# Attention with a mixture of experts on one Trainium2 core: row sums of squares moved from ScalarE's accumulator to two halvings on GpSimd and a reduction on VectorE

## The chip, the core and the metric

The kernel runs on one core of one Trainium2 chip. The metric is the device time of one execution in microseconds; a lower one is better. The kernel before took 217.38 us (median of 3 runs, 215.89 to 218.58).

The core's engines run side by side, each through its own list of instructions in the order in which the program wrote it. TensorE (PE in the profile) multiplies matrices into the banks of PSUM. ScalarE (ACT) and VectorE (DVE) read PSUM and SBUF. GpSimd (POOL) works on SBUF alone and issues the indirect DMAs. SyncE (SP) issues the other DMAs. Engines wait for one another by semaphores; an engine that waits holds up all that stands behind the waiting instruction in its list.

## The reference

```python
x = L0_attn_x                                        # (8, 512, 128), f32
mod = (_silu(L0_c) @ L0_wmod).reshape(8, 6, 1, -1)   # sa, ca, ga, sb, cb, gb
h = _layernorm(x) * (1 + ca) + sa
x = x + ga * attn(h)
h = _layernorm(x) * (1 + cb) + sb
x = x + gb * ffn(h)                                  # top-1 routing to 16 experts, 128 -> 512 -> 128

# attn(x), with rms_norm(x) = x * rsqrt(mean(x * x, axis=-1) + eps)
qkv = einsum('btd,ed->bte', rms_norm(x), w_qkv)
q, k, v = split(qkv, 3, axis=-1)
q, k = rms_norm(q), rms_norm(k)
w = exp(k); kv = w * v
y = sigmoid(q) * cumsum(kv, axis=1) / (cumsum(w, axis=1) + 1e-06)
u, g = split(einsum('bte,fe->btf', y, w_swiglu), 2, axis=-1)
return x + einsum('btd,ed->bte', u * silu(g), w_out)
```

The change touches one thing in it: the sums of squares of q and of k over their 128 channels, which the rms_norm of q and k needs.

## The kernel before

The work is 8 batches of 512 tokens; a batch is four tiles (`NJ` = 4) of 128 tokens. The attention and the routing of all batches come first and end with the scatter of the routed rows to DRAM (`scatter`, L495, 32 indirect DMAs on GpSimd). Eight pairs of experts follow, which this change doesn't touch; they start when all rows are scattered.

In the attention part each engine has a list of calls `name(b)` written out by hand, b being the batch (GpSimd L510 to L517, ScalarE L652 to L673, VectorE L926 to L951, TensorE L1193 to L1215). Batches overlap in these lists. The chain of one batch is:

1. `normalize1(b)` (GpSimd or VectorE) gives the normed rows, `transpose1(b)` (TensorE) transposes them to bank 2, and `modulate1(b)` (ScalarE or VectorE, L301) scales and shifts them into `hT`, 128 channels by 512 tokens.
2. `squares(b)` (GpSimd, L482) squares `hT`, and `h_square_sums(b)` (TensorE, L1025) sums the squares; `h_means(b)` (VectorE, L742) reads them.
3. `project_qk(b)` (TensorE, L1033) fills banks 0 and 1 with q and k: for each tile j 128 columns of q and 128 of k, so a bank holds two tiles. There is one such pair of banks, and `project_qk(b+1)` waits until `exp_q(b)` has read it.
4. `square_sums(b)` (ScalarE, L554) makes `ssq`, the eight sums of squares of every row, and `qk_means(b)` (VectorE, L751) makes `nrm` of them (one instruction, L754).
5. `rms_scales(b)` (ScalarE, L564) takes `nrm` through Ln and Exp; `exp_k(b)` and `exp_q(b)` (ScalarE, L571, L580) read q and k from PSUM with these scales.
6. `transpose_k`, `transpose_q`, `weigh_v`, `transpose_kv`, the cumulative sums `scan_w` and `scan_kv` (VectorE), `denominator`, `log_denominator`, `reciprocal` and `weigh_sums` (GpSimd or VectorE, L271) give y.
7. `project_g`, `project_u`, `clamp_g`, `exp_g`, `log_g`, `sigmoid_g`, `silu`, `gate_u`, `project_out` and `residual` end the attention; the second layer norm, the logits, `count_seen` and `slots` lead to `scatter(b)`.

`square_sums(b)` before is eight pairs, one for each half tile:

```python
last = act.activation(junk[:, 2 * j + m, :], ps_qk[:, j, m * D:(m + 1) * D],
                      ACT.Square, accum_out=ssq[:, j, m:m + 1])
```

Each pair is an ACTIVATE of 128x128 and an ACTIVATION_READ_ACCUMULATOR of 128x1. TensorE's list has a few multiplications without use (`run_early`, `run_late`) that fill gaps. The order on GpSimd around the change is `squares(0); normalize1(1); squares(1); weigh_sums(0); squares(2); silu(0); squares(3); normalize1(4); squares(4); normalize1(5); squares(5); weigh_sums(3); silu(2); count_seen(0); normalize1(6); scatter(0); squares(6); normalize1(7)` and so on.

Of the kernel before, what the change touches and what calls it, by code (L numbers as in the profile page):

```python
# [5 lines left out]
def adaln_attention_moe(  # L6
# [30 lines left out]
    ALU = mybir.AluOpType  # L37
    ACT = mybir.ActivationFunctionType
    X = mybir.AxisListType.X
# [23 lines left out]
    with ctx:  # L63
# [3 lines left out]
        def sem(name):  # L67
            return ctx.enter_context(nc.semaphore(name))
# [129 lines left out]
        yw = junk[:, 0:NS, :]  # L198
        x_tiles = x_all[:, :, :, :].rearrange("p b j d -> p (b j) d")
# [35 lines left out]
        pool_past = sem("pool_past")  # L235
        last_sent = sem("last_sent")
# [222 lines left out]
        def _(pool):  # L459
# [22 lines left out]
            def squares(b):  # L482
                after(pool, hT_done, b)
                after(pool, mh_ps, b, 1)
                pool.tensor_tensor(hsq[:, :], hT[b % NHT][:, :], hT[b % NHT][:, :], ALU.mult  # L485
                                   ).then_inc(hsq_done, 1)

            def count_seen(b):

                after(pool, oh_done, b)  # L490
                after(pool, rank_ps, b)
                pool.tensor_tensor(seen[:, :, :], seen[:, :, :], oh[b % 2][:, :, :], ALU.add
                                   ).then_inc(seen_done, 1)
# [16 lines left out]
            squares(0); normalize1(pool, 1); squares(1); weigh_sums(pool, 0)  # L510
            squares(2); silu(pool, 0); squares(3); normalize1(pool, 4); squares(4)
            normalize1(pool, 5); squares(5); weigh_sums(pool, 3); silu(pool, 2); count_seen(0)
            normalize1(pool, 6); scatter(0); squares(6); normalize1(pool, 7); silu(pool, 3)
            weigh_sums(pool, 4); squares(7); count_seen(1); scatter(1); weigh_sums(pool, 5)
# [29 lines left out]
        def _(act):  # L544
# [9 lines left out]
            def square_sums(b):  # L554
                after(act, nrm_b, b, 1)
                for j in range(NJ):
                    if j % 2 == 0:
                        after(act, qk_ps, 2 * b + j // 2)
                    for m in range(2):
                        last = act.activation(junk[:, 2 * j + m, :], ps_qk[:, j, m * D:(m + 1) * D],  # L560
                                              ACT.Square, accum_out=ssq[:, j, m:m + 1])
                last.then_inc(ssq_done, 1)
# [91 lines left out]
            reciprocal(0); rms_scales(1); exp_k(1); exp_q(1); keep_row(0); ln1_scale(3); exp_g(0)  # L654
            log_g(0); sigmoid_g(0); keep_row(1); modulate1(act, 3); log_denominator(1); square_sums(2)
            ln1_scale(4); reciprocal(1); rms_scales(2); exp_k(2); exp_q(2); exp_g(1); ln2_scale(0)
            keep_row(2); log_g(1); sigmoid_g(1); square_sums(3); ln1_scale(5); rms_scales(3); exp_k(3)
            exp_q(3); keep_row(3); log_denominator(2); reciprocal(2); square_sums(4)
            log_denominator(3); modulate2(act, 0); rms_scales(4); exp_k(4); exp_g(2); exp_q(4)
# [59 lines left out]
        def _(dve):  # L719
# [31 lines left out]
            def qk_means(b):  # L751
                after(dve, ssq_done, b)
                dve.wait_ge(nrm_a, b + 1)
                dve.scalar_tensor_tensor(nrm[:, 0:2 * NJ].rearrange("p (j m) -> p j m", m=2), ssq[:, :, :],  # L754
                                         1.0 / D, mh[:, :].unsqueeze(2).to_broadcast([P, NJ, 2]),
                                         ALU.mult, ALU.add).then_inc(nrm_b, 1)
# [171 lines left out]
            normalize1(dve, 2); scan_kv(0); h_means(1); qk_means(1); modulate1(dve, 2); diagonal(0); aggregate1(3)  # L928
# [3 lines left out]
            clamp_g(1); scan_w(2); modulate1(dve, 4); weigh_v(2); aggregate1(5); shift2(0); stats1(6)  # L932
            silu(dve, 1); gate_u(1); qk_means(3); denominator(2); h_means(4); shift1(5)
            normalize2(dve, 0); scan_kv(2); residual(1); scan_w(3); weigh_sums(dve, 2)
            modulate1(dve, 5); denominator(3); weigh_v(3); qk_means(4); clamp_g(2); stats2(1)
# [432 lines left out]
```

## Time and profile before

| what | us |
|---|---|
| median of 3 runs | 217.38 |
| lowest and highest | 215.89, 218.58 |
| span of the profiled execution | 217.0 |
| attention and routing, up to the last scatter's issue | 0 to 129.4 |
| experts | some 130 to 217 |

The profile is one execution. Its span runs from the first to the last instruction and lies 0.4 us under the median of the runs. PE is TensorE's matrix multiplications (their ends are modelled, so a busy PE isn't PE at its peak), PEld its loads of weights. A row of the timeline has the start in us, the duration in us, the engine, the line, the operation, output and input, the count, and in brackets the idle time of the engine before it with what ended that. Consecutive instructions of an engine can overlap at their ends, so the distance of two starts is the price in a list, and is a little less than the duration.

### The profile page before, as it was taken

Reading aid. Unit: us, or ns where it says so; the run is one execution under the profiler, and the core shown is the slowest. Engines: PE = TensorE matmul, PEld = TensorE weight load, DVE = VectorE, ACT = ScalarE, POOL = GpSimd, SP = SyncE. Lnnn points to the kernel's source line nnn. Section 1 sums busy time; section 2 is a strip of 40 time slices with the busy share of each in tenths; the row PEclk is TensorE's granted clock in tenths of the full one; section 3 lists DMA queues with packets and bytes.
Section 4 is the critical chain, followed back from the end, with each engine's and each line's share of the span. In section 5 each row is a group of like instructions: output and inputs, shape, how many; then the busy total and the mean of one; then the engine's idle time right before and its main releaser. Section 6 shows DMA issues by size and latency. Waiting matters only on the chain.

```text
span 217.0 us, 4034 instructions
## 1 busy us (share of the span) xinstructions
PE 192.2 (89%) x1177; PEld 155.3 (72%) x1177; DVE 153.2 (71%) x476; ACT 145.0 (67%) x425; POOL 113.8 (52%) x139
## 2 busy tenths in 40 slices
PE   6999599999999979999988749999999999999930
PEld 4789377788879759775665414888878889788830
DVE  3657999999999999999996407156847668485430
ACT  4494868999999979987756641574855848555300
POOL 6311504431387828577767760002754378487774
PEclk9788999999999999999999996999999999999996
DMA  5999999507905013114453216999879585321000
GB/s 149 285 343 360 355 360 309 222 5 215 270 21 177 0 53 147 48 73 138 161 186 119 99 65 159 362 358 357 277 254 283 168 268 157 85 100 46 31 30 20
DMA packets 37284, 38.60 MB, mean 178 GB/s; under 512 B 2591, under 2 KB 31334, under 8 KB 37264
## 3 DMA queue, kind: packets, MB, share of 16 engines
q1 hardware_dynamic: 33936, 31.29, 46.1%
q0 software_dynamic: 3328, 7.07, 9.1%
q8 instruction: 9, 0.15, 0.3%
q14 instruction: 11, 0.09, 0.1%
HBM read 19.19 MB, written 18.95 MB: 176 GB/s over the span
## 4 chain that ended last, share of the span: by engine, by line
PE 59%; DVE 17%; issue 8%; POOL 7%; ACT 4%; DMA 2%; POOLq 1%; SPq 0%; DVEq 0%
PE bank L1280 14%; PE bank L1266 11%; PE bank L1039 5%; POOL out_dram L529 4%; PE bank L1083 3%; PE bank L1109 3%; PE bank L1057 3%; PE bank L1092 2%; PE bank L1078 2%; PE bank L1094 2%; PE bank L1050 2%; DVE kvsum L780 2%; PE bank L1327 2%; PE bank L1237 2%; DVE rows L804 2%
## 5 line engine op out<-in xcount | busy, mean ns | idle before, releaser
L529 POOL DMA_INDIRECT out_dram<-x_all,rest x40 | 43.2, 1080 | 42.2 <-DVE x_all L985 23.8
L503 POOL DMA_INDIRECT dispatched_rows<-rows,slot x32 | 32.2, 1006 | 16.0 <-issue 9.0
L709 ACT ACTIVATE HT<-bank 128x320 f32<-128x320 f32 x64 | 28.0, 438 | 10.2 <-PE bank L1266 9.8
L1280 PE MATMUL bank<-HT,w 128*128 128x320 f32 x112 | 32.4, 432 | 0.0
L1280 PEld LDWEIGHTS bank<-HT,w 128*128 128x128 f32 x112 | 20.6, 189 | 6.7
L1266 PE MATMUL bank<-xth,w1h 128*128 128x320 f32 x64 | 22.6, 353 | 0.2 <-DVE xtl L961 0.2
L955 DVE TENSOR_TENSOR w1l<-w,w1h 128x1024 fp32r<-128x1024 f32 x8 | 16.1, 2022 | 7.4 <-DMA dispatched_rows<-rows,slot 7.4
L1004 DVE COPY OT<-bank 128x320 f32<-128x320 f32 x14 | 6.9, 492 | 18.5 <-PE bank L1280 18.5
L1266 PE MATMUL bank<-xth,w1l 128*128 128x320 f32 x64 | 19.8, 309 | 0.0
L1266 PE MATMUL bank<-xtl,w1h 128*128 128x320 f32 x64 | 19.8, 309 | 0.0
L560 ACT ACTIVATE junk<-bank 128x128 f32<-128x128 f32 x64 | 16.5, 288 | 1.5 <-PE bank L1039 1.3
L485 POOL TENSOR_TENSOR hsq<-hT 128x512 f32<-128x512 f32 x8 | 9.3, 1164 | 15.2 <-ACT hT L308 9.6
L1039 PE MATMUL bank<-wqkvT,hT 128*128 128x256 f32 x64 | 16.5, 405 | 0.0
L681 ACT CAST w1h<-w 128x1024 fp32r<-128x1024 f32 x8 | 16.3, 2044 | 0.0
L694 ACT CAST xth<-bank 128x640 fp32r<-128x640 f32 x7 | 4.8, 692 | 15.8 <-PE bank L1237 15.8
L977 DVE SCALAR_TENSOR_TENSOR junk<-bank,rest 128x128 f32<-128x128 f32 x40 | 11.5, 345 | 5.4 <-PE bank L1299 3.6
L1057 PE MATMUL bank<-ident,ewkv 128*128 128x128 f32 x96 | 14.7, 280 | 0.0
L1057 PEld LDWEIGHTS bank<-ident,ewkv 128*128 128x128 f32 x96 | 11.9, 148 | 3.8 <-issue 2.2
L277 POOL TENSOR_TENSOR yT<-kvsum,rden 128x512 f32<-128x512 f32 x6 | 7.6, 1273 | 13.0 <-ACT rden L596 12.5
L1039 PEld LDWEIGHTS bank<-wqkvT,hT 128*128 128x128 f32 x64 | 12.7, 206 | 2.4 <-issue 0.5
L560 ACT ACTIVATION_READ_ACCUMULATOR junk<-bank 128x1 f32 x64 | 14.2, 222 | 0.0
L1092 PE MATMUL bank<-diag_ga,hT 128*128 128x128 f32 x64 | 12.8, 282 | 0.6 <-DVE GT L800 0.6
(172 smaller groups left out, 494.1 us busy)
## 6 DMA issues: line engine op xcount, KB each, us to landing
w<-in_L_ffn_w_dram SPq DMA_DIRECT2D x16, 512.0 KB, 7.6
dispatched_rows<-blank SPq DMA_DIRECT2D x8, 965.0 KB, 13.2
rest<-dispatched_rows SPq DMA_DIRECT2D x8, 645.0 KB, 6.4
hin<-dispatched_rows SPq DMA_DIRECT2D x7, 320.0 KB, 7.5
x_all<-in_L_attn_x_dram SPq DMA_DIRECT2D x8, 256.0 KB, 5.2
rows<-gb_row SPq DMA_DIRECT2D x8, 256.0 KB, 3.8
out_dram<-rows SPq DMA_DIRECT2D x8, 256.0 KB, 3.2
out_dram<-x_all,rest POOLq DMA_INDIRECT x40, 2.3
```

Source lines behind the costliest of these rows:

```text
L503: pool.indirect_dma_start(out=disp_d, out_offset=bass.IndirectOffsetOnAxis(ap=slot[:, b, j:j + 1], axis=0), in_=rows[:, b, j, :], in_offse ...
L529: pool.indirect_dma_start(out=out_d.rearrange("b t d -> (b t) d"), out_offset=bass.IndirectOffsetOnAxis(ap=rest[i % RING][:, n, C_TOK - D: ...
L560: last = act.activation(junk[:, 2 * j + m, :], ps_qk[:, j, m * D:(m + 1) * D], ACT.Square, accum_out=ssq[:, j, m:m + 1])
L681: act.copy(w1h[i % 2][:, :, :, :], w1[i % RING][:, :, :].rearrange("p e (m f) -> p e f m", f=NF)).then_inc(w1h_done, 1)
L709: act.activation(HT[e][:, f, :], ps_h[c % HB][:, 0:CAP], ACT.Gelu_apprx_tanh).then_inc(h_done, 1)
L955: dve.tensor_tensor(w1l[i % 2][:, :, :, :], w1[i % RING][:, :, :].rearrange("p e (m f) -> p e f m", f=NF), w1h[i % 2][:, :, :, :].bitcast( ...
L977: last = dve.scalar_tensor_tensor(yw[:, n, :], ROWS[n] if i == LAST else ps_y[:, n * D:(n + 1) * D], rest[i % RING][:, n, C_PROB - D:C_PRO ...
L1039: last = pe.matmul(ps_qk[:, j, :], hT[b % NHT][:, j * P:(j + 1) * P], wqkvT[:, 0:2 * D], start=True, stop=True)
L1057: last = pe.transpose(ps[:, j * P:(j + 1) * P], t[:, j, m, :], ident[:, :])
L1092: pe.matmul(ps_u[:, j * P:(j + 1) * P], hT[b % NHT][:, j * P:(j + 1) * P], diag_ga[:, b, :], start=True, stop=False)
L1266: last = pe.matmul(ps_h[c % HB][:, 0:CAP], w[i % 2][:, e, f, :], x[i % 2][:, e * CAP:(e + 1) * CAP], start=(n == 0), stop=(n == 2))
L1280: last = pe.matmul(ps_o[e], w2[i % RING][:, e, f, :], HT[e][:, f, :], start=(f == 0), stop=(f == NF - 1))
```

## The change

It does two things.

`square_sums(b)` no longer uses the accumulator. ScalarE squares a whole bank at a time (two ACTIVATEs of 128x512 instead of eight pairs) into `junk`, which then holds 8 rows of 128 squares in each partition. GpSimd's new `fold_squares(b)` adds the upper 64 of each row to the lower 64, waits for that, and adds the upper 32 to the lower 32. `qk_means(b)` on VectorE first reduces 8 rows of 32 to `ssq` (a new TENSOR_REDUCE), waits for it, and then goes on as before. `fold_squares(b)` has its place written out in GpSimd's list.

`modulate1(b)` for b = 2, 4 and 5 moves from VectorE's list to ScalarE's: for 2 it stands between `reciprocal(0)` and `rms_scales(1)`, for 4 between `ln2_scale(0)` and `keep_row(2)`, for 5 between `square_sums(4)` and `log_denominator(3)`. TensorE's list and SyncE's are the same.

```diff
+        squared = junk[:, :, :].rearrange("p (h n) d -> p h (n d)", h=2)
...
+        sqr_done = sem("sqr_done")
+        fold_a, fold_b = sem("fold_a"), sem("fold_b")
...
+            def fold_squares(b):
+
+                after(pool, sqr_done, b)
+                pool.tensor_tensor(junk[:, :, 0:64], junk[:, :, 0:64], junk[:, :, 64:128], ALU.add
+                                   ).then_inc(fold_a, 1)
+                pool.wait_ge(fold_a, b + 1)
+                pool.tensor_tensor(junk[:, :, 0:32], junk[:, :, 0:32], junk[:, :, 32:64], ALU.add
+                                   ).then_inc(fold_b, 1)
...
-            squares(0); normalize1(pool, 1); squares(1); weigh_sums(pool, 0)
-            squares(2); silu(pool, 0); squares(3); normalize1(pool, 4); squares(4)
-            normalize1(pool, 5); squares(5); weigh_sums(pool, 3); silu(pool, 2); count_seen(0)
-            normalize1(pool, 6); scatter(0); squares(6); normalize1(pool, 7); silu(pool, 3)
-            weigh_sums(pool, 4); squares(7); count_seen(1); scatter(1); weigh_sums(pool, 5)
+            squares(0); normalize1(pool, 1); fold_squares(0); squares(1); fold_squares(1); weigh_sums(pool, 0)
+            squares(2); silu(pool, 0); fold_squares(2); squares(3); normalize1(pool, 4); squares(4)
+            fold_squares(3); normalize1(pool, 5); fold_squares(4); squares(5); weigh_sums(pool, 3)
+            silu(pool, 2); fold_squares(5); count_seen(0); normalize1(pool, 6); scatter(0); squares(6)
+            normalize1(pool, 7); fold_squares(6); silu(pool, 3); weigh_sums(pool, 4); squares(7)
+            count_seen(1); scatter(1); fold_squares(7); weigh_sums(pool, 5)
...
             def square_sums(b):
-                after(act, nrm_b, b, 1)
-                for j in range(NJ):
-                    if j % 2 == 0:
-                        after(act, qk_ps, 2 * b + j // 2)
-                    for m in range(2):
-                        last = act.activation(junk[:, 2 * j + m, :], ps_qk[:, j, m * D:(m + 1) * D],
-                                              ACT.Square, accum_out=ssq[:, j, m:m + 1])
-                last.then_inc(ssq_done, 1)
+                after(act, ssq_done, b, 1)
+                for half in range(2):
+                    after(act, qk_ps, 2 * b + half)
+                    last = act.activation(squared[:, half, :], bank01[:, half * 512:(half + 1) * 512], ACT.Square)
+                last.then_inc(sqr_done, 1)
...
-            reciprocal(0); rms_scales(1); exp_k(1); exp_q(1); keep_row(0); ln1_scale(3); exp_g(0)
+            reciprocal(0); modulate1(act, 2); rms_scales(1); exp_k(1); exp_q(1); keep_row(0); ln1_scale(3); exp_g(0)
...
-            keep_row(2); log_g(1); sigmoid_g(1); square_sums(3); ln1_scale(5); rms_scales(3); exp_k(3)
+            modulate1(act, 4); keep_row(2); log_g(1); sigmoid_g(1); square_sums(3); ln1_scale(5); rms_scales(3); exp_k(3)
...
-            log_denominator(3); modulate2(act, 0); rms_scales(4); exp_k(4); exp_g(2); exp_q(4)
+            modulate1(act, 5); log_denominator(3); modulate2(act, 0); rms_scales(4); exp_k(4); exp_g(2); exp_q(4)
...
             def qk_means(b):
-                after(dve, ssq_done, b)
+                after(dve, fold_b, b)
+                dve.tensor_reduce(ssq[:, :, :].rearrange("p j m -> p (j m)"), junk[:, :, 0:32], X, ALU.add
+                                  ).then_inc(ssq_done, 1)
+                dve.wait_ge(ssq_done, b + 1)
                 dve.wait_ge(nrm_a, b + 1)
...
-            normalize1(dve, 2); scan_kv(0); h_means(1); qk_means(1); modulate1(dve, 2); diagonal(0); aggregate1(3)
+            normalize1(dve, 2); scan_kv(0); h_means(1); qk_means(1); diagonal(0); aggregate1(3)
...
-            clamp_g(1); scan_w(2); modulate1(dve, 4); weigh_v(2); aggregate1(5); shift2(0); stats1(6)
+            clamp_g(1); scan_w(2); weigh_v(2); aggregate1(5); shift2(0); stats1(6)
...
-            modulate1(dve, 5); denominator(3); weigh_v(3); qk_means(4); clamp_g(2); stats2(1)
+            denominator(3); weigh_v(3); qk_means(4); clamp_g(2); stats2(1)
```

## Rows read from the trace of the kernel before

**Rows 1.** Windows: stretch, length, busy us of PE, PEld, DVE, ACT, POOL, granted clock, DMA.
```profile
16.00:18.00 2.00, 2.00 (x11) 2.00 (x10) 0.89 (x1) 1.22 (x4) 1.04 (x1) 0.50 1.06 362
...
41.00:49.00 8.00, 8.00 (x53) 6.69 (x52) 7.91 (x28) 7.65 (x34) 2.93 (x5) 1.00 0.06 20
...
60.00:70.00 10.00, 9.99 (x73) 8.56 (x71) 9.65 (x37) 9.90 (x39) 8.01 (x12) 1.00 0.31 108
...
14.00:98.00 84.00, 78.52 (x535) 64.83 (x534) 78.95 (x262) 72.85 (x276) 40.82 (x51) 0.98 0.55 179
```
**Rows 2.** Waits, 10 to 140 us: us in total, times, longest.
```profile
PE bank L1190 <- DVE diag_ga L920: 2.1, 1, 2.1
PE bank L1083 <- DVE rows L804: 2.0, 3, 1.5
...
ACT nrl L566 <- DVE nrm L754: 1.0, 3, 0.5
```
**Rows 3.** Timeline of ScalarE, batches 1, 3 to 5.
```profile
20.92 0.26 ACT L560 ACTIVATE junk<-bank 128x128 f32<-128x128 f32 x1
...
22.91 0.68 ACT L596 ACTIVATE rden<-lden 128x512 f32<-128x512 f32 x1
...
47.11 1.16 ACT L584 ACTIVATE ewkv<-bank,nrr 128x128 f32<-128x128 f32 x4
...
49.30 0.63 ACT L596 ACTIVATE rden<-lden 128x512 f32<-128x512 f32 x1
49.84 0.26 ACT L560 ACTIVATE junk<-bank 128x128 f32<-128x128 f32 x1
...
63.37 0.24 ACT L566 ACTIVATE nrl<-nrm 128x12 f32<-128x12 f32 x1
...
63.84 0.78 ACT L308 ACTIVATE hT<-bank,mod 128x512 f32<-128x512 f32 x1
64.52 1.13 ACT L576 ACTIVATE ewkv<-bank,nrr 128x128 f32<-128x128 f32 x4
```
**Rows 4.** Groups by line in 0 to 140 us: busy us, mean ns of one.
```profile
L284 POOL TENSOR_TENSOR gs<-gc,sg 128x512 f32<-128x512 f32 x4 | 5.1, 1272 | 5.4 <-ACT sg L612 5.3
...
L794 DVE TENSOR_SCALAR gc<-bank 128x512 f32<-128x512 f32 x8 | 5.5, 685 | 0.6 <-issue 0.3 <-PE bank L1078 0.2
...
L831 DVE TENSOR_REDUCE mx<-bank 128x4 f32<-128x64 f32 x8 | 1.7, 219 | 1.9 <-PE bank L1109 1.8
...
L649 ACT COPY gb_row<-bank 128x512 f32<-128x512 f32 x2 | 1.2, 600 | 0.0
```
**Rows 5.** Timeline of GpSimd, four places, and the last scatter.
```profile
33.50 1.04 POOL L485 TENSOR_TENSOR hsq<-hT 128x512 f32<-128x512 f32 x1
...
60.77 1.76 POOL L294 TENSOR_SCALAR xh<-x_all,rs,nm 128x128 f32<-128x128 f32 x4
...
68.12 1.05 POOL L485 TENSOR_TENSOR hsq<-hT 128x512 f32<-128x512 f32 x1
...
73.80 1.04 POOL L485 TENSOR_TENSOR hsq<-hT 128x512 f32<-128x512 f32 x1
...
128.45 0.97 POOL L503 DMA_INDIRECT dispatched_rows<-rows,slot  x1 [0.30 <-issue]
```
**Rows 6.** Timeline of VectorE: the sums' consumer in batches 1 and 6, and a diagonal.
```profile
23.11 0.17 DVE L754 SCALAR_TENSOR_TENSOR nrm<-ssq,mh 128x8 f32<-128x8 f32 x1 [0.41 <-ACT junk L560]
...
23.91 2.11 DVE L920 TENSOR_TENSOR diag_ga<-ident,mod 128x1024 f32<-128x1024 f32 x1
...
73.86 1.02 DVE L754 SCALAR_TENSOR_TENSOR nrm<-ssq,mh 128x8 f32<-128x8 f32 x1
```
**Rows 7.** Timeline of TensorE: two sums of squares of h, and the projection of batch 4.
```profile
36.27 0.95 PE L1029 MATMUL bank<-tri,hsq 128*128 128x1 f32 x8
...
48.41 1.96 PE L1039 MATMUL bank<-wqkvT,hT 128*128 128x256 f32 x8
...
69.59 0.95 PE L1029 MATMUL bank<-tri,hsq 128*128 128x1 f32 x8
```

## Prediction

> **What bounds the kernel now.** I read the windows by stage first. In 14 to 98 us, where the change lies, TensorE is busy 78.5 of 84 us, VectorE 79.0, ScalarE 72.9 and GpSimd only 40.8 [rows 1]. That invites moving work to GpSimd. The single stages say more: in 41 to 49 us TensorE has 8.00 of 8, VectorE 7.91 and ScalarE 7.65, in 60 to 70 us 9.99, 9.65 and 9.90 of 10 [rows 1]. Three engines are full at once, each through a list in fixed order. Such a kernel is bound by the chain that passes from list to list, and an engine's total is not its limit. The waits say the same: few are long, and ScalarE waits for VectorE's `nrm` for 1.0 us in all [rows 2]. So the sums of squares are now made just in time for what needs them. Nor is GpSimd free everywhere: in 60 to 70 us it is busy 8.01 of 10 us [rows 1], as the first scatter lies there. After the attention the experts wait for the last scatter, issued at 128.45 us [rows 5]. They take the rest of the span whatever came before, so a delay of the attention is a delay of the kernel.
>
> **Prices, one batch.** On ScalarE the eight pairs last from 20.92 to 22.91 us, 1.99 us [rows 3]. A 128x512 read of a bank has a mean of 0.60 us there, and successive starts of that size lie 0.54 us apart (49.30 to 49.84) [rows 3, 4]. Two Squares then cost 1.04 to 1.2; I take 1.04, so ScalarE's list gets 0.95 us shorter, 7.6 us over eight batches. Three modulations come onto it at 0.68 us each (63.84 to 64.52) [rows 3]: +2.0. VectorE gives about as much for those three and takes on eight reductions.
>
> The path is another matter. Before, from the first square to the start of `nrm` it was 23.11 - 20.92 = 2.19 us [rows 3, 6]. Now come the Squares (1.1 to the end of the second), two folds and a reduction, with a semaphore between each.
> - First fold, 512 outputs from two inputs: GpSimd's nearest row has 1.27 [rows 4]; with both inputs the same tile it has 1.04 [rows 5]. I take 1.27, since the two halves are different data, and 1.04 as the lower bound.
> - Second fold, 256 outputs: not in the trace. Below it lies a 128x128 instruction at 1.76 / 4 = 0.44 [rows 5], above it 1.27. I take 0.7, nearer the lower end, since it has half the elements.
> - Reduction of 256 to 8: below 0.22 (64 elements), above 0.69 (512) [rows 4]; on the line between them 0.42.
> - Four hand-overs between engines or behind a semaphore at some 0.07 each, worked out from 63.37 + 0.24 to 63.84 and the like: 0.25.
>
> The sum is 1.1 + 1.27 + 0.7 + 0.42 + 0.25 = 3.75, 1.55 longer than before. The bounds give 3.1 (0.9 longer) and 4.6 (2.4 longer). Seen from ScalarE, `rms_scales(b)` can start 2.85 us after its last Square (with 0.2 for `nrm`), less what its list has in between. The Trainium skill (GPSIMD Engine Reference, section 3.1) gives a two-input elementwise instruction about 2.6 cycles for each element on GpSimd; taking 256 elements off the 1.27 by that rule, an estimate of mine for the second fold is 0.72, and the sum would be the same.
>
> **One more price: the port.** `nrm` reads two SBUF tiles and has 0.17 us in batch 1 but 1.02 in batch 6, started at 73.86, just behind GpSimd's squares at 73.80 and ended with them [rows 5, 6]. So it stands still while GpSimd reads. After the change the instruction in front of which GpSimd finished its fold is exactly what sets `nrm` free, and GpSimd goes on at once with `weigh_sums`, `squares` or `silu` (1.04 to 1.27); the reduction hides 0.45 of that, so `nrm` is 0.6 to 0.8 later wherever GpSimd has such work ready: batches 1, 2, 4, 6, 7. The Trainium skill (SBUF — State Buffer, section "Who interferes with whom") states it as a rule: a VectorE instruction with two SBUF inputs blocks against a GpSimd instruction that reads SBUF for the whole of it, and a reduction doesn't. The trace agrees for `nrm`; no row here has a reduction against GpSimd.
>
> **The walk.** I followed the lists by hand, with each instruction behind the last of its waits and the trace's durations kept. Delays against before:
> - Batch 0 has nothing between `square_sums` and `rms_scales`. VectorE stands until the folds are done; +1.0 at 20 us, as part of it ran in ScalarE's idle time.
> - Batch 1: the modulation and `reciprocal(0)` cover 1.2 of 2.85. VectorE's `diagonal(0)`, which ended at 26.0 [rows 6] and for which TensorE stood 2.1 us [rows 2], waits for `nrm`, and `weigh_sums(0)` behind the fold blocks it further: +0.6, together 1.6.
> - Batch 2: `squares(3)` ran at 33.50 on GpSimd and TensorE took it at 36.27, so it had 1.7 us to spare [rows 5, 7]. Now it stands behind `fold_squares(2)`, which waits for Squares that end at about 36.3. Folds to 38.3, squares to 39.4, TensorE stands until then: 36.27 becomes 39.5. +1.6, together 3.2. All queued behind on TensorE (project_g(1), project_qk(3)) goes with it.
> - Batch 3: only `ln1_scale` (0.47, like the pair 63.37 to 63.84) [rows 3] lies between: 2.85 - 0.47 - 0.2 of old wait - 0.95 saved = +1.2, together 4.4. The exp_q that starts at 47.11 ends at 48.27, and TensorE's project_qk(4) starts at 48.41 [rows 3, 7]. There is no slack in that loop: 48.4 becomes 52.8.
> - Batch 4: modulate1(5), a logarithm and a modulate2 cover 1.9; with the port and the moved instruction +0.7, together 5.1.
> - Batch 5: `normalize1(6)` ran at 60.77, beside the squares [rows 5]. Now it is behind `fold_squares(5)` and `count_seen(0)`, and starts at about 68.4: +7.7. After it stand scatter(0) with its four DMAs and squares(6), which goes from 68.12 to some 75.7; TensorE's 69.59 becomes 76.8 [rows 5, 7]. modulate1(6) (63.84) [rows 3] waits for the transpose of normalize1(6), so ScalarE is held up too. +2.0, together 7.1.
> - Batch 6: ScalarE has over 3 us of other work in between. The fold lies in front of `silu(3)` and `weigh_sums(4)`, whose delay TensorE's old wait for `residual` (1.5) [rows 2] takes up. +0.
> - Batch 7: `log_denominator` alone (0.54) is cover: +1.3, with `weigh_sums(5)` on the port +0.7; together 9.1.
> - The tail has small waits of several engines (of the 2.0 of TensorE for `residual`, 0.5 is left) [rows 2]: I give back 1.1.
>
> Sum: +8.0. The profiled span is 217.0, so 225.0; the median is 0.4 above the span: 225.4. SyncE's transfers are issued as before; the first experts' weights are in long before. Where I cost the reductions on VectorE at nothing beyond the path, it is because VectorE is waiting for the folds at that point; otherwise eight of them less three modulations cost 8 x 0.45 - 3 x 0.72 = 1.4 us.
>
> **Rivals.**
> 1. ScalarE is the bound and the folds are covered. For it: ScalarE has 9.90 of 10 us in 60 to 70 us [rows 1], and all of its squares there follow the instruction before without a gap. Then 7.6 - 2.0 = 5.6 us come off: 211.8. It decides if `rms_scales(b)` finds `nrm` ready, that is if 2.85 us of other work stands before it in the list; that holds in one batch of eight. Chance 0.10.
> 2. Gains and waits cancel: the folds at their lower bounds (path +0.9), and GpSimd's order costs nothing since VectorE or ScalarE is later there anyway. ScalarE's 2.85 becomes 2.2 and batch 3's +1.2 becomes +0.6; four such batches (0, 1, 3, 7) give 2.4: 219.8. Chance 0.08.
> 3. Only the list of ScalarE counts, not that of GpSimd: the batch 2 and 5 terms (3.6) drop out: 221.8. Against it: squares(3)'s margin of 1.7. Chance 0.12.
> 4. More than forecast: TensorE's clock. After its early waits it was granted 0.50 in 16 to 18 us, the level of 1.2 GHz, though the 2.1 us for which TensorE waited for the diagonal [rows 2] left the mean of 14 to 98 us at 0.98 [rows 1]. New waits of 1 to 2 us could bring two such stretches, each costing about 2: 229.5. The upper bounds of the folds (0.85 more in five batches) give the same. Chance 0.10.
> 5. The forecast, 221.8 to 229: chance 0.60.
>
> **How the numbers follow.** 2% is 4.3 us, so slower begins at 221.7, which is also about what a measurement of this kernel can tell. Slower: 0.60 + 0.10 + half of rival 3 = 0.76. Within 2%: 0.08 + 0.06 = 0.14. Faster: 0.10. The range reaches from 220, which leaves out rivals 1 and 2, to 231 (the upper bounds and a little clock).
>
> **What would show it.** ScalarE's idle time in front of L566's counterpart should be some 10 us in all, released by VectorE's `nrm`; VectorE's in front of the reduction some 8, released by the second fold; TensorE's sum of squares of batch 3 should stand at about 39.5 and wait for GpSimd; project_qk(4) at about 52.8; the last scatter at about 136.5. Squares under 1.2 us a batch and folds of 1.27 and 0.7 show the prices. I am wrong if those waits are there but the last scatter is not later (then the chain was elsewhere), or if the folds take under 1.5 us together.

## The result, and the profile after

The changed kernel took 234.44 us (median of 4 runs, 231.73 to 235.33), the kernel before 217.98 beside it (4 runs, 215.89 to 219.60). The ratio is 1.073, with an interval of 1.0665 to 1.0795: slower by 16.5 us at the medians, 15.9 by the ratio, where +8.0 was forecast. Ratios leave disturbed runs out (of the kernel after, the profiled one of 235.33 us), so what one kernel costs over another is taken from ratios below, at 218 us for 1.00, and can differ by an us or two from the medians shown. The profiled execution has a span of 233.2 us, 16.2 over the 217.0 of before.

The groups by line in 0 to 146 us (busy us, mean ns of one, then idle time before them and its releaser) stand against [rows 3, 4, 6]:

```profile
L494 POOL TENSOR_TENSOR junk<-junk 128x512 f32<-128x512 f32 x8 | 10.1, 1267 | 14.5 <-ACT junk L571 14.5
...
L571 ACT ACTIVATE junk<-bank 128x512 f32<-128x512 f32 x16 | 8.8, 586 | 3.1 <-PE bank L1052 3.1
...
L497 POOL TENSOR_TENSOR junk<-junk 128x256 f32<-128x256 f32 x8 | 5.8, 723 | 0.6
...
L767 DVE SCALAR_TENSOR_TENSOR nrm<-ssq,mh 128x8 f32<-128x8 f32 x8 | 3.9, 484 | 0.3
...
L763 DVE TENSOR_REDUCE ssq<-junk 128x8 f32<-128x256 f32 x8 | 3.3, 418 | 5.5 <-POOL junk L497 5.3
...
L576 ACT ACTIVATE nrl<-nrm 128x12 f32<-128x12 f32 x8 | 1.7, 210 | 14.8 <-DVE nrm L767 14.8
```

The prices are those of the forecast: 1.27, 0.72 and 0.42 us, and two Squares within 1.06. The last row is where the chain shows: ScalarE stands 14.8 us for `nrm`, against 1.0 before [rows 2]. GpSimd stands as long, 14.5 us, for the Squares, and all that is queued behind the first fold stands with it. The waits in 10 to 146 us (total, times, longest) tell who pays for that on TensorE, against [rows 2]:

```profile
PE bank L1091 <- POOL yT L280: 3.2, 2, 2.0
...
PE bank L1042 <- POOL hsq L488: 2.7, 2, 1.9
PE bank L1203 <- DVE diag_ga L933: 2.6, 1, 2.6
...
ACT rden L606 <- POOL yT L280: 2.2, 1, 2.2
```

GpSimd's timeline and TensorE's show one of these places, the sum of squares of batch 3, as [rows 5, 7] do for before:

```profile
39.81 1.27 POOL L494 TENSOR_TENSOR junk<-junk 128x512 f32<-128x512 f32 x1 [3.49 <-ACT junk L571]
41.16 0.72 POOL L497 TENSOR_TENSOR junk<-junk 128x256 f32<-128x256 f32 x1
41.84 1.04 POOL L488 TENSOR_TENSOR hsq<-hT 128x512 f32<-128x512 f32 x1
```
```profile
28.32 2.08 PE L1203 MATMUL bank<-diag_ga,wout 128*128 128x512 f32 x2 [2.59 <-DVE diag_ga L933]
30.18 1.91 PE L1091 MATMUL bank<-yT,wswT 128*128 128x512 f32 x2
31.89 1.91 PE L1096 MATMUL bank<-yT,wswT 128*128 128x512 f32 x2
...
42.93 1.05 PE L1042 MATMUL bank<-tri,hsq 128*128 128x1 f32 x8 [1.94 <-POOL hsq L488]
...
88.44 2.05 PE L1091 MATMUL bank<-yT,wswT 128*128 128x512 f32 x2 [1.97 <-POOL yT L280]
```

`squares(3)` needs nothing of the folds, yet it stands behind two of them and behind the 3.5 us for which the first waits. TensorE stands 1.94 us for it. Behind each of the three waits something further happens, which the windows show (columns as in [rows 1]; the granted clock is the figure after POOL's):

```profile
24.00:28.00 4.00, 1.13 (x8) 0.97 (x8) 2.50 (x6) 1.70 (x6) 3.92 (x4) 0.88 1.06 361
28.00:32.00 4.00, 3.68 (x5) 1.62 (x6) 3.58 (x14) 2.81 (x11) 1.16 (x1) 0.50 1.06 358
...
44.00:48.00 4.00, 4.00 (x11) 1.89 (x12) 2.00 (x12) 1.60 (x7) 1.19 (x3) 0.57 0.00 0
...
88.00:92.00 4.00, 3.56 (x11) 2.53 (x12) 2.85 (x10) 2.98 (x10) 1.64 (x3) 0.57 0.00 2
...
132.00:136.00 4.00, 3.96 (x21) 2.45 (x21) 2.84 (x12) 2.27 (x6) 2.83 (x4) 0.61 0.41 148
```

In 28 to 32 us TensorE is busy 3.68 of 4 us but does 5 multiplications: its granted clock is 0.50, the level of 1.2 GHz. In the timeline above, two pairs of 128x512 start 1.71 us apart (30.18, 31.89). At full clock they start 0.86 apart (23.82 and 24.68, in e2's timeline below). So these three waits cost themselves, and then about as much again in slow multiplications. A fourth slow stretch, at 132 us, stands behind a wait of 1.39 us. Not every such wait has one behind it: before's of 2.1 us for the diagonal [rows 2] ended at 26.07, and its windows of 24 to 28 and 28 to 32 us both have 1.00.

How the delay grew, against the forecast and against a version with the clock kept (run e3, below), in us:

| mark | before | forecast | after | e3 |
|---|---|---|---|---|
| sum of squares of batch 3 starts | 36.27 | 39.5 | 42.93 | 38.23 |
| project_qk(4) starts | 48.41 | 52.8 | 58.19 | 51.95 |
| normalize1(6) on GpSimd starts | 60.77 | 68.4 | 73.80 | 67.62 |
| sum of squares of batch 6 starts | 69.59 | 76.8 | 82.02 | 75.84 |
| last scatter is issued | 128.45 | 136.5 | 145.63 | 137.74 |

From that issue to the end of the span it is 88.6 us before, 87.6 after and 88.2 in e3, so the delay is made in the attention. (The 129.4 of the table of stages is where that last instruction ends.)

### The profile page after: what moved, and what is told of

Same layout as the page of the kernel before. It is cut to its first block, busy times and chain, and to the rows that moved or that the text cites. A ratio compares the mean times of both kernels' runs of the same rounds, so it can differ in the third digit from the quotient of the medians.

```text
span 233.2 us, 3946 instructions
## 1 busy us (share of the span) xinstructions
PE 199.6 (86%) x1177; PEld 158.7 (68%) x1177; DVE 158.0 (68%) x481; ACT 139.2 (60%) x316; POOL 129.5 (56%) x155
## 4 chain that ended last, share of the span: by engine, by line
PE 48%; DVE 14%; POOL 14%; issue 11%; ACT 8%; DMA 2%; POOLq 1%; DVEq 0%; ACTq 0%
PE bank L1293 13%; PE bank L1279 11%; POOL out_dram L542 4%; POOL junk L494 4%; PE bank L1052 4%; PE bank L1091 3%; PE bank L1096 3%; ACT junk L571 2%; PE bank L1203 2%; POOL dispatched_rows L515 2%; DVE w1l L968 2%; POOL junk L497 2%; PE bank L1250 2%; DVE ewkv L776 2%; DVE rows L817 1%
## 5 line engine op out<-in xcount | busy, mean ns | idle before, releaser
L494 POOL TENSOR_TENSOR junk<-junk 128x512 f32<-128x512 f32 x8 | 10.1, 1267 | 14.5 <-ACT junk L571 14.5
L1052 PE MATMUL bank<-wqkvT,hT 128*128 128x256 f32 x64 | 17.0, 413 | 0.5 <-ACT ewkv L594 0.5
L1070 PE MATMUL bank<-ident,ewkv 128*128 128x128 f32 x96 | 14.5, 278 | 2.4 <-ACT ewkv L586 2.4
L1091 PE MATMUL bank<-yT,wswT 128*128 128x512 f32 x16 | 11.3, 798 | 3.5 <-POOL yT L280 3.2
L1105 PE MATMUL bank<-diag_ga,hT 128*128 128x128 f32 x64 | 13.3, 290 | 0.0
L1279 PEld LDWEIGHTS bank<-xth,w1h 128*128 128x128 f32 x64 | 12.1, 188 | 1.3 <-DVE xtl L974 0.6
```

The costliest lines, as they stand in the source:

```text
L494: pool.tensor_tensor(junk[:, :, 0:64], junk[:, :, 0:64], junk[:, :, 64:128], ALU.add).then_inc(fold_a, 1)
L1052: last = pe.matmul(ps_qk[:, j, :], hT[b % NHT][:, j * P:(j + 1) * P], wqkvT[:, 0:2 * D], start=True, stop=True)
L1070: last = pe.transpose(ps[:, j * P:(j + 1) * P], t[:, j, m, :], ident[:, :])
L1091: pe.matmul(ps_g, wswT[:, D:2 * D], yT[:, :], start=True, stop=True).then_inc(g_ps, 1)
L1105: pe.matmul(ps_u[:, j * P:(j + 1) * P], hT[b % NHT][:, j * P:(j + 1) * P], diag_ga[:, b, :], start=True, stop=False)
L1279: last = pe.matmul(ps_h[c % HB][:, 0:CAP], w[i % 2][:, e, f, :], x[i % 2][:, e * CAP:(e + 1) * CAP], start=(n == 0), stop=(n == 2))
```

## The experiments

Theories: *path*, the chain from the Squares through the folds to `nrm` is longer and ScalarE waits for it; *list*, what counts is the useful work on GpSimd behind a fold that waits; *clock*, the new waits lower TensorE's clock; *port*, GpSimd's reads of SBUF hold VectorE up. A diff against the kernel before is marked so; the others are against the kernel after. "Before" is the median of its runs beside each experiment.

### The three modulations

**e1**: they go back to VectorE.

```diff
-            reciprocal(0); modulate1(act, 2); rms_scales(1); exp_k(1); ...
+            reciprocal(0); rms_scales(1); exp_k(1); ...
...
-            normalize1(dve, 2); scan_kv(0); h_means(1); qk_means(1); diagonal(0); aggregate1(3)
+            normalize1(dve, 2); scan_kv(0); h_means(1); qk_means(1); modulate1(dve, 2); diagonal(0); aggregate1(3)
```
(batches 4 and 5 alike)

> The changed kernel with the three modulations back in VectorE's list; squares, folds and reduction stay. Path theory (the 3.75 us from the first square to nrm makes the delay, wherever the modulations are): ScalarE gets 2.0 us shorter, VectorE 2.1 us longer while it mostly waits for folds; the time stays within 1.5 us of the changed kernel's 234. Rival (the modulations overload ScalarE in batches 4 and 5): 3 us or more come off, 231 or less. Clock theory: TensorE's long waits are for the diagonal, for squares(3) and for weigh_sums(4), none of which this takes away, so the three stretches at half clock stay.

Measured 233.29 us (233.06 to 236.24), ratio 1.0774 [1.0658, 1.0889]; before 218.20. ScalarE waits 15.7 us for `nrm`, not 14.8. The modulations aren't what made the kernel slow. This kernel is before with the squares, folds and reduction alone, and they cost 16.9 us. The expectation that the three slow stretches stay fell at one of them. TensorE waits for `squares(3)` exactly as long as in the kernel after, and what follows runs at full clock, where the kernel after had 0.57 and 11 multiplications:

```profile
42.63 1.05 PE L1042 MATMUL bank<-tri,hsq 128*128 128x1 f32 x8 [1.94 <-POOL hsq L488]
```
```profile
44.00:48.00 4.00, 4.00 (x25) 3.07 (x24) 3.56 (x12) 3.00 (x11) 0.89 (x3) 1.00 0.00 0
```

**e2**, the reverse: the kernel before with these three moves alone and no folds.

> The kernel before with only the three modulations moved to ScalarE; accumulator sums stay. Path theory: nothing lengthens the path to nrm; ScalarE's list gets 2.0 us longer, part of it in idle time, so 217 to 219. Rival (ScalarE is full, so the move costs its price and more): 220 or more. If VectorE was the bound, 215 to 216.

Measured 216.29 us (214.44 to 218.69, 10 runs), ratio 0.9912 [0.9865, 0.9959]; before 218.20. It is 0.9% under before, less than the 2% that counts as faster here. TensorE's timeline shows one place: the row product that waited 2.1 us for the diagonal [rows 2] follows almost at once, since VectorE no longer has `modulate1(2)` in front of `diagonal(0)`:

```profile
23.82 1.02 PE L1083 MATMUL bank<-yT,wswT 128*128 128x512 f32 x2
24.68 1.02 PE L1190 MATMUL bank<-diag_ga,wout 128*128 128x512 f32 x2
25.53 0.95 PE L1029 MATMUL bank<-tri,hsq 128*128 128x1 f32 x8
```

But most of the lead of this profiled execution is older than that place. The sum of squares of batch 1 starts at 18.01 us here and at 21.03 before, that of batch 3 at 32.24 and 36.27: 3.0 of the 4.0 us lie ahead of the first moved instruction. There the two kernels have the same lists, but before's execution had a low clock (before first, then e2):

```profile
8.00:12.00 4.00, 4.00 (x13) 3.18 (x12) 1.84 (x12) 2.45 (x13) 2.77 (x5) 0.57 1.07 295
```
```profile
8.00:12.00 4.00, 3.68 (x23) 3.13 (x22) 2.30 (x17) 3.22 (x21) 2.77 (x5) 1.00 1.07 297
```

So the moves leave about 1 us in the profile and 1.9 by the runs, of which some may be the clock (mean 0.977 over e2's runs, 0.969 over before's beside them). With the folds in place they show no gain beyond the noise (1.0774 in e1 against 1.073). The other half of the change, the folds, costs the 17.

### A shorter path

**e5**, one fold, and VectorE reduces 8 rows of 64:

```diff
-                                   ).then_inc(fold_a, 1)
-                pool.wait_ge(fold_a, b + 1)
-                pool.tensor_tensor(junk[:, :, 0:32], junk[:, :, 0:32], junk[:, :, 32:64], ALU.add
...
-                dve.tensor_reduce(ssq[...], junk[:, :, 0:32], X, ALU.add
+                dve.tensor_reduce(ssq[...], junk[:, :, 0:64], X, ALU.add
```

> The changed kernel with one halving instead of two: GpSimd adds the upper 64 to the lower 64, VectorE reduces 8 rows of 64 (about 0.69 instead of 0.42 us). The path from the squares to nrm gets 0.72 + 0.07 - 0.27 = 0.5 us shorter, GpSimd's list 5.8 us shorter over eight batches, VectorE's 2.1 us longer. Path theory: of eight batches six or so pay, so 3 to 4 us come off: 230 to 231.5. Order theory (GpSimd's occupancy counts too): up to 5, 229 to 231. VectorE as bound: no gain, 234 or more.

Measured 224.27 us (223.88 to 227.15), ratio 1.0334 [1.0233, 1.0436]; before 217.91. **e6**, no fold at all, VectorE reduces 8 rows of 128:

```diff
-                after(pool, sqr_done, b)
-                pool.tensor_tensor(...)   (both folds)
+                pass
...
-                after(dve, fold_b, b)
-                dve.tensor_reduce(ssq[...], junk[:, :, 0:32], X, ALU.add
+                after(dve, sqr_done, b)
+                dve.tensor_reduce(ssq[...], junk[:, :, :], X, ALU.add
```

> The changed kernel without folds: ScalarE squares by the bank as in the change, VectorE reduces 8 rows of 128 itself (about 1.1 to 1.2 us). GpSimd's list is that of before. The path from the first square to nrm is 1.1 + 1.2 + 0.2 = 2.5 us, 0.3 more than before, and VectorE has 8 x 1.15 - 2.1 = 7.1 us more than before. Path theory (the two folds and what stands behind them are the cause): most of the delay goes, 218 to 223, the rest being VectorE's longer list. Rival (bank-wide squares or VectorE's extra work are the cause): 228 or more. The accumulator's saving on ScalarE as a gain: under 216.

Measured 223.56 us (222.61 to 224.38), ratio 1.0261 [1.0177, 1.0345]. The reductions of the two, by line (e5's first):

```profile
L760 DVE TENSOR_REDUCE ssq<-junk 128x8 f32<-128x512 f32 x8 | 5.4, 681 | 1.8 <-POOL junk L494 1.8
```
```profile
L758 DVE TENSOR_REDUCE ssq<-junk 128x8 f32<-128x1024 f32 x8 | 9.7, 1208 | 0.0
```

The step from two folds to one shortens the path by 0.72 less 0.26 (681 - 418 ns) and a hand-over, some 0.5 us a batch: 4 us at most, if all eight batches counted. It gave 8.6 (1.073 to 1.0334). ScalarE still waits 11.8 us for `nrm` in e5, not 14.8. The path theory thus explains less than half of the gain. The mean granted clock points to the rest: 0.966 over e5's runs against 0.946 over those of after. As it has two levels, 0.50 and 1.00, that is some 15 against 25 us at the lower one, and 10 us at half clock cost 5 at most, an estimate of mine. And with no fold at all this sum still loses 5.7 us to the accumulator. I put that down to the reduction of 1.2 us plus hand-overs on VectorE, which was full already, but no run isolates it.

### The folds by themselves

Four kernels built on the kernel before, whose sums stay on ScalarE's accumulator. GpSimd gets work on a tile of its own that nobody reads, at the places where the folds stand after the change. They compute all of the reference; the work is extra, as is one memset of 0.95 us near the start that fills the tile.

**e7**: both folds, and the first waits until ScalarE's sums of that batch are done, as the real one does; `nrm` doesn't wait for them.

```diff
(against before)
...
+            def fold_squares(b):
+
+                after(pool, ssq_done, b)
+                after(pool, fold_b, b, 1)
+                pool.tensor_tensor(spare[:, :, 0:64], spare[:, :, 0:64], spare[:, :, 64:128], ALU.add
+                                   ).then_inc(fold_a, 1)
+                pool.wait_ge(fold_a, b + 1)
+                pool.tensor_tensor(spare[:, :, 0:32], spare[:, :, 0:32], spare[:, :, 32:64], ALU.add
+                                   ).then_inc(fold_b, 1)
```

> The kernel before, with its accumulator sums, to which GpSimd's two folds a batch are added at the change's places in its list, on a spare tile of zeros, started when the sums are there; nobody waits for them and nothing of the output depends on them. Path theory: only what stands behind the folds on GpSimd and the port are left of the change: 219 to 223. If GpSimd's occupancy were all of it: 228 or more. If it were nothing: within 1 us of the kernel before run beside it.

Measured 238.46 us (234.64 to 239.02), ratio 1.0845 [1.0708, 1.0983]; before 217.91. The path theory fell here: nobody waits for a fold, and the kernel is 18.4 us slower than before, at least as slow as the one after the change (the intervals overlap). Its waits in 10 to 146 us show the order on GpSimd's list at work:

```profile
POOL spare L497 <- ACT junk L576: 18.8, 8, 4.2
...
PE bank L1094 <- POOL yT L280: 6.1, 3, 3.1
...
PE bank L1045 <- POOL hsq L490: 5.2, 2, 3.5
```

**e8**: e7, and `nrm` waits for the second fold too (`after(dve, fold_b, b)` in place of `ssq_done` in `qk_means`).

> As the one before, but VectorE's nrm waits for the second fold: accumulator sums on ScalarE (2.0 us a batch) and the folds as a pure delay of 2.05 us in the path, modulations on VectorE as before, no reduction. Against the changed kernel ScalarE has 7.6 us more in its list and the path is 2.19 + 2.1 = 4.3 instead of 3.75. Path theory: slower than the changed kernel, 236 to 240. Rival (the accumulator's removal gained nothing since ScalarE waits anyway, and the path's end is what counts from the last square: 2.05 + 0.2 here against 2.65 there): 230 to 234.

Measured 244.02 us (243.57 to 245.52), ratio 1.1207 [1.1114, 1.1300]. By the ratios the wait of `nrm` adds 7.9 us to the 18.4 of e7, give or take 3 to 4, as e7's runs scatter.

**e9**: e7 without `after(pool, ssq_done, b)`: the folds start as soon as their turn comes.

> As the kernel before with two folds a batch on a spare tile at the change's places in GpSimd's list, but they no longer wait for the sums: they run as soon as GpSimd reaches them. Left of the change are only the 8 x 2 us of occupancy and the port. Waiting theory (what costs is that useful work stands in GpSimd's list behind a fold that waits for ScalarE): 218 to 222. Occupancy theory (the 16 us on GpSimd or their reads of SBUF against VectorE's are what costs): 228 or more.

Measured 223.49 us (222.08 to 225.58), ratio 1.0236 [1.0130, 1.0343]; before 218.43. **e10**: as e9, but each fold is a memset of 128x1024, which takes nearly the same time (0.95 us each, 1.90 a batch, against 1.99) and reads nothing:

```diff
-                pool.tensor_tensor(spare[:, :, 0:64], spare[:, :, 0:64], spare[:, :, 64:128], ALU.add
-                                   ).then_inc(fold_a, 1)
+                pool.memset(spare[:, :, :], 0.0).then_inc(fold_a, 1)
```
(and the second alike)

> As the one before with two memsets of 128x1024 (about 1 us each) in place of the two folds: the same time on GpSimd, but no reads of SBUF. Port theory (VectorE's instructions with two SBUF inputs stand still while GpSimd reads): 1 to 2 us less than with the free folds. If only GpSimd's time counts: the same within 1 us.

Measured 219.03 us (217.67 to 221.57, 10 runs), ratio 1.0023 [0.9983, 1.0062]. The groups of `nrm`, e9 first:

```profile
L769 DVE SCALAR_TENSOR_TENSOR nrm<-ssq,mh 128x8 f32<-128x8 f32 x8 | 3.4, 424 | 0.3 <-ACT junk L575 0.2
```
```profile
L767 DVE SCALAR_TENSOR_TENSOR nrm<-ssq,mh 128x8 f32<-128x8 f32 x8 | 1.3, 157 | 0.3 <-ACT junk L573 0.2
```

These four make a ladder. The time that the folds occupy GpSimd costs 0.5 us, inside the noise. That they read SBUF costs 4.6 more: the same `nrm` takes 424 ns beside folds and 157 beside memsets, 2.1 us in all, and another small VectorE instruction with two SBUF inputs, layer norm's `nm`, takes 1.6 us more. That the first waits, with useful work queued behind it, costs 13.3 more. That `nrm` waits as well costs 7.9. From there, giving up the accumulators and moving the modulations brings back 10.4. The steps hold in this order; another order was not run. The two upper ones contain slow multiplications too: the mean clock over the runs is 0.974 in e10, 0.966 in e9, 0.933 in e7 and 0.918 in e8. The Trainium skill (SBUF — State Buffer, section "Who interferes with whom") says that a VectorE instruction with two SBUF inputs contends with a GpSimd instruction that reads SBUF and not with one that only writes it; by that rule e10's `nrm` is as quick as without GpSimd, and the rows agree.

### The clock

**e3**: the kernel after, with 13 multiplications without use that run while TensorE waits for the diagonal, for `squares(3)` and for `yT` of batch 4.

```diff
             def h_square_sums(b):
-                after(pe, hsq_done, b)
                 claim(pe, "v", nrm_a, b)
+                if b == 3:
+                    for _ in range(4):
+                        pe.matmul(bank3[:, 0:256], tri[:, 0:P], tri[:, 0:256], start=True, stop=True)
+                after(pe, hsq_done, b)
```
(four alike in `project_g(4)`, five ahead of the first row product)

> The changed kernel with 13 multiplications without use (128x256, some 0.43 us each at full clock) inside three waits of TensorE: 5 in front of the first row product (wait 2.6 us), 4 in front of the sums of squares of batch 3 (1.9), 4 in front of project_g(4) (2.0). Nothing else moves. Clock theory: TensorE keeps 1.00 in the three stretches that now have 0.50 to 0.57 (28 to 34, 44 to 47, 88 to 91 us), and 5 to 6 us come off: 228 to 229. Path theory alone (the clock costs nothing, as other engines bind): within 1 us of 234.

Measured 230.12 us (227.77 to 230.75), ratio 1.0593 [1.0505, 1.0680]; before 218.20. The windows of the profiled execution at the same places:

```profile
24.00:28.00 4.00, 3.56 (x13) 2.17 (x12) 3.86 (x14) 2.79 (x11) 3.15 (x2) 1.00 1.06 358
28.00:32.00 4.00, 4.00 (x26) 2.92 (x25) 4.00 (x11) 2.31 (x6) 0.00 (x0) 1.00 1.06 360
...
124.00:128.00 4.00, 4.00 (x21) 2.72 (x21) 2.39 (x12) 2.23 (x6) 2.80 (x4) 0.59 0.39 144
```

From the first row product to the sum of squares behind it the kernel after took 34.60 - 28.32 = 6.28 us, e3 29.84 - 26.30 = 3.54 for the same work. This stretch costs 2.7 us. The next, from the sum of squares of batch 3 to project_qk(3), is 6.18 (42.93 to 49.11) against 4.46 (38.23 to 42.69): 1.7. The low clock of 124 to 128 us, the counterpart of the one at 132 in the kernel after, was left. In this execution all marks came within 1.3 us of the forecast (the table above). It is the fastest of the four; the others had mean clocks of 0.945 to 0.954 and took 229.5 to 230.8, so the fills don't keep the clock each time. By the ratio they gain 3.0 us, less than the 5 to 6 of the expectation.

**e13**: 27 such multiplications, at five more waits (`transpose1(6)`, `h_square_sums(5)`, `transpose_k(0)` and `(3)`, `project_g(5)`).

> The changed kernel with the 13 multiplications in TensorE's waits and 14 more (5 in front of transpose_k(0), 2 of transpose_k(3), 3 of transpose1(6), 2 of project_g(5), 2 of the sums of squares of batch 5). Clock theory in full (half of the 16 us are TensorE at half clock behind waits): 226 to 228, mean clock 0.975 or more up to the last scatter. Clock already paid by the first 13 (what is left are the waits themselves): 229 to 231, as with 13.

Measured 227.31 us (226.44 to 229.93), ratio 1.0424 [1.0328, 1.0520]; before 218.49. The fills give back about 7 us (1.073 to 1.0424 is 6.7), with the order of the lists unchanged. What remains, 9.2 over before, is near the forecast. But 7 is not the clock's share of the change, as before has its own slow multiplications, in 8 to 20 us (0.50 in 16 to 18 [rows 1]), where after and e13 have none. The mean clocks, 0.946 over the runs of after, 0.967 to 0.970 over those of before and 0.976 over those of e13, make some 25, 13 to 14 and 11 us at the lower level. So the change adds about 11 us at half clock, which cost 5.5 to 6 at most (an estimate from these means), and some 10 us are left for waits and port.

### The order on GpSimd

**e4**: three pieces of useful work go ahead of the fold that blocked them.

```diff
-            squares(2); silu(pool, 0); fold_squares(2); squares(3); normalize1(pool, 4); squares(4)
+            squares(2); silu(pool, 0); squares(3); fold_squares(2); normalize1(pool, 4); squares(4)
...
-            normalize1(pool, 7); fold_squares(6); silu(pool, 3); weigh_sums(pool, 4); squares(7)
-            count_seen(1); scatter(1); fold_squares(7); weigh_sums(pool, 5)
+            normalize1(pool, 7); silu(pool, 3); weigh_sums(pool, 4); fold_squares(6); squares(7)
+            count_seen(1); scatter(1); weigh_sums(pool, 5); fold_squares(7)
```

> The changed kernel with three folds moved back in GpSimd's list: squares(3) in front of fold_squares(2), silu(3) and weigh_sums(4) in front of fold_squares(6), weigh_sums(5) in front of fold_squares(7). The number of instructions and their prices stay. Order theory (what stands behind a waiting fold on GpSimd costs 1.6 us in batch 2, about 2 in batch 6 and 1.2 in batch 7, and the waits in batches 2 and 6 also drop the clock): 228 to 230, with full clock at 44 to 47 and 88 to 91 us. Path theory alone: the folds only change places with the instructions behind them and nrm comes later by as much: 232 to 235.

Measured 231.44 us (229.78 to 231.57), ratio 1.0621 [1.0527, 1.0716]; before 218.20. **e14** is its first line alone, **e15** its second and third.

> The changed kernel with squares(3) in front of fold_squares(2), nothing else. The forecast's own term for this was 1.6 us. If it is right, 232 to 233; with the clock that the wait of 1.9 us costs afterwards, 230.5 to 231.5; if nrm of batch 2, which now comes later by GpSimd's squares where they collide, takes it back, 234.

> The changed kernel with silu(3) and weigh_sums(4) in front of fold_squares(6) and weigh_sums(5) in front of fold_squares(7), nothing else. The forecast gave batch 6 nothing and batch 7 1.3 + 0.7. If batch 6 did cost (ScalarE waits 2.2 us for GpSimd's yT and TensorE 2.0), 230 to 232; if the forecast was right on it, 233 to 234.

e14 took 230.86 us (228.74 to 232.03), ratio 1.0578 [1.0475, 1.0681]; e15 233.27 (232.99 to 235.96), ratio 1.0736 [1.0636, 1.0836]; before 218.49. Against the kernel after, e4 gains 2.4 us, e14 3.3 and e15 nothing (1.0736 against 1.073). So the one swap of `squares(3)` carries the whole gain; the sum of squares of batch 3 then starts at 37.95 and waits for nothing, and 40 to 44 and 44 to 48 us have 1.00. Yet the mean clock of e14's runs is no higher than that of after (0.948 and 0.946), and its profiled execution has slow stretches in 12 to 20, 60 to 64 and 84 to 88 us. The clock thus gives little of the 3.3.

In e15 `project_g(4)` starts at 84.83, not 88.44, and TensorE's wait for `yT` is gone. But it comes back one instruction later. The fold of batch 6 is now the later one, VectorE stands 1.98 us for it in front of its reduction, `gate_u`'s `GT` stands behind that in VectorE's list, and TensorE waits for `GT`, with a low clock again behind it (0.68 in 88 to 92 us):

```profile
88.25 0.46 PE L1105 MATMUL bank<-diag_ga,hT 128*128 128x128 f32 x2 [2.31 <-DVE GT L813]
```

In the kernel after this instruction started at 90.28, which is 8.26 us behind the sum of squares of batch 6; here it is 8.02 (80.23 to 88.25).

**e12** joins e3 and e4, **e11** joins e5 with both.

> The changed kernel with both folds, the three folds later in GpSimd's list and the 13 multiplications. Clock and order as separate terms: 234 - 4 - 2.5 = 227.5. Order mainly through the clock: 229 to 230, no better than either alone.

> The changed kernel with one halving only, the three folds later in GpSimd's list, and the 13 multiplications in TensorE's waits. If the parts add up from the changed kernel (one fold about -9, fills about -4, later folds about -2.5), it comes to 219 to 221, where the path of 3.25 us is all that is left. If they are the same delay seen three times (a wait of TensorE that drops the clock), 222 to 225.

e12 took 229.29 us (228.48 to 230.28), ratio 1.0519 [1.0453, 1.0585]; e3's gain of 0.0137 and e4's of 0.0109 would give 1.0484 if they added, which lies inside, so e12 doesn't tell the two expectations apart. e11 took 225.89 (224.58 to 226.18), ratio 1.0328 [1.0259, 1.0397], where e5 alone has 1.0334 and all three added would have 1.009. With one fold, fills and order thus have nothing more to give; I read it so that once a wait is short, there is no slow stretch behind it for the others to save, which no run isolates.

## Why the prediction was wrong in size

The direction was right, and these steps came out:
- **Prices.** Squares 1.06 (1.04 taken), folds 1.27 and 0.72 (1.27 and 0.7), reduction 0.42 (0.42). The path of batch 1 was 26.37 - 22.68 = 3.69 (3.75). The estimate from the Trainium skill (GPSIMD Engine Reference, section 3.1), 0.72 for the second fold, agrees with its mean of 723 ns. (A hand-over of 0.07 doesn't follow from the row named for it, since 63.37 to 63.84 holds two instructions of ScalarE; in batch 1 of the kernel after the four measured 0.03 to 0.08, so the term held.)
- **The port.** `nrm` took 0.75 to 0.77 us in batches 1, 6 and 7 and 0.52 to 0.53 in 2 and 4, against 0.17 when free: 0.6 later in three of the five batches named, and 0.35 in two, where 0.6 to 0.8 was forecast. e9 and e10 show the cause.
- **Waits, in kind.** ScalarE waited for `nrm` and VectorE for the folds, and `h_square_sums(3)` for GpSimd. The sizes were off: 14.8 us where "some 10" stood, and 5.3 where 8 stood.
- **The walk, with the clock kept.** In the profiled execution of e3 the last scatter is issued at 137.74, forecast 136.5. The sum of +8.0 stands against e13's 9.2. In part that is luck. The walk started from before's trace with its low clock in 8 to 20 us, which cost that execution about 3 us by e2's marks and which e3's and e13's didn't have. Terms that failed, below, are in the sum as well, and e3's profile is of its fastest run.

These failed:
- **Rival 4 was kept apart from the sum.** The walk kept "the trace's durations", among them TensorE's at 2.4 GHz, though the walk itself made TensorE wait at three places. The reason was before's wait of 2.1 us, which left the clock at 1.00; behind the new ones it fell. Rival 4 had 0.10 and two stretches of about 2 us. In the profiled execution three came in the attention and a fourth in its tail, on top of the waits: two of them measured 2.7 and 1.7. Fills gave back 6.7 us in e13, and the mean clocks put the change's own share at 5.5 to 6 at most. That is most of the 8 us that were missing (15.9 by the ratio against 8.0). The range fell with it: 231 left room for "a little clock".
- **Batch 2's term.** 1.6 was the wait alone, which measured 1.94. Undone in e14 it is worth 3.3, though the spread of the runs reaches from about 1 to 5.5. In the profiled execution of the kernel after the wait and the slow work behind it make 1.94 + 1.7 = 3.6. But the mean clock of e14's runs is no higher, so that this is the split isn't shown.
- **Batch 6 at +0.** I held that the delay of `silu(3)` and `weigh_sums(4)` goes into an old wait of TensorE. But ScalarE's `reciprocal(5)` also waits for `weigh_sums(4)` (2.16 us, at 88.48), and its `rms_scales(6)` stands behind that in its list: it starts at 89.16, though `nrm` was there at 87.2. So the step missed a wait. TensorE's old wait didn't take the delay up either: it stood 1.97 us for `yT`, with a slow stretch behind it. What all this is worth isn't shown, as in e15 the fold held `GT` up instead and nothing was gained.
- **Which wait counts.** The sum went mostly through `nrm` (batches 0, 1, 3, 4 and 7) and took GpSimd's order as a matter of batches 2 and 5; rival 3 even had it at nothing. By the ladder a fold that nobody waits for costs 18.4 us, and letting `nrm` wait for it adds 7.9. The walk came near the sum without the clock, but it would have sent one to shorten the path, which by the ladder is the smaller part.

What stays open: how exactly the 16 us divide between waits, clock and port, as each measure took away parts of the others, and before had slow multiplications of its own in another place; why the clock falls behind one wait of 1.94 us and not behind the same wait in e1; whether path and clock are all of the 8.6 us that one fold less brings, with no single stretch named; and which marks of e3 would hold in its slower runs.

## What to carry to other kernels

When three engines are full through lists in fixed order, an idle engine isn't free to take a step of their chain: ask first what stands behind the new instruction in its list, and put that ahead of it or leave the step where it is. Count a new wait of some 2 us on TensorE as up to twice its length when the work behind it is multiplications, and put that into the range: here three of them were followed by slow work, and two in other executions (2.1 us in before, 1.94 in e1) were not. And split a change that has several parts: here one alone was 0.9% faster than before, and the other cost 17 us.

## What was unexpected of the hardware

- In the kernel after slow stretches came behind waits of 1.94 to 2.6 us, and the two that were measured cost 1.7 and 2.7 us. The same wait of 1.94 us at the same place had a slow stretch behind it in the kernel after (0.57 in 44 to 48 us) and none in e1 (1.00).
- Within one kernel the time mostly follows the mean granted clock: three runs of after had 235.00 us at 0.929, 233.89 at 0.940 and 231.73 at 0.962, but the fourth had 235.33 at 0.953.
- Two memsets of 0.95 us a batch on GpSimd cost 0.5 us in all, inside the noise, and two additions of 1.99 us a batch, equally unawaited, 5.1.
